# The order of ScalarE's second phase in a causal attention: the outputs' copy and the turned half's copy each go one place ahead

## The reference, cut to what matters

```
q, k, v per head (16 heads of 64), v and k from a latent of 64; rotary on q and k
scores = q @ k.T / 8, causal mask
probs  = softmax(scores)
out    = probs @ v                  # per head
x      = layernorm(x + out @ wo)
```

## Time and profile before

| | us |
|---|---|
| median of three runs | 1637.8 (1637.06 to 1641.13) |
| profiled execution | 1635.31 |
| its span, first to last instruction | 1633.2 |
| TensorE busy in the span | 1504.0 (92%) |
| VectorE, ScalarE busy | 1146.4 (70%), 1087.7 (67%) |
| GpSimd busy | 523.0 (32%) |
| TensorE busy between 41 and 434 us, steps 1 to 30 of the first attention | 375.77 of 393 |

### The profile page before, as it was taken

The page is one execution under the profiler, slowest core; times in us unless marked ns, Lnnn a source line. Parts: engine busy times, 40 slices in busy tenths (PEclk is TensorE's granted clock), DMA queues, the critical chain, the costliest instruction groups (busy, mean ns, idle before and its releaser), DMA issues. The chain is left out here.

```text
span 1633.2 us, 30449 instructions
## 1 busy us (share of the span) xinstructions
PE 1504.0 (92%) x9934; PEld 1018.6 (62%) x9934; DVE 1146.4 (70%) x2592; ACT 1087.7 (67%) x2499; POOL 523.0 (32%) x476
## 2 busy tenths in 40 slices
PE   7999999999979999999998999997999988999986
PEld 6777777777657888888863333333666655566654
DVE  2677777676657777777787888864777753777755
ACT  3565665656567888888865777754778754787852
POOL 1222222222231122221110000014777733677732
PEclk9999999999979999999997999977999998999998
DMA  7000000000002212212100000000000000000000
GB/s 244 2 2 1 0 0 0 0 0 0 1 28 80 78 64 77 76 52 77 65 1 1 1 1 1 1 1 0 2 1 1 1 1 0 1 2 1 1 1 26
DMA packets 18849, 36.54 MB, mean 22 GB/s; under 512 B 5492, under 2 KB 10736, under 8 KB 16560
## 3 DMA queue, kind: packets, MB, share of 16 engines
q1 hardware_dynamic: 18752, 35.29, 6.4%
HBM read 34.10 MB, written 1.18 MB: 22 GB/s over the span
## 5 line engine op out<-in xcount | busy, mean ns | idle before, releaser
L915 DVE TENSOR_TENSOR m_hidp<-m_hid,m_hidp 128x512 fp32r<-128x512 f32 x256 | 178.2, 722 | 77.9 <-ACT m_hidp L831 76.6
L305 ACT ACTIVATE a_prob<-a_prob,a_negmax 128x512 f32<-128x512 f32 (+3 forms) x256 | 142.2, 556 | 135.9 <-DVE a_negmax L382 135.9
L836 ACT ACTIVATE m_hid<-ps,pre_w 128x512 f32<-128x512 f32 x256 | 175.3, 685 | 63.5 <-PE ps L1064 62.7
L1064 PE MATMUL ps<-c_sb_st,m_w1p 128*128 128x512 f32 x768 | 191.4, 398 | 0.0
L1119 PE MATMUL ps<-m_hidp,m_w2p 128*128 128x512 f32 x768 | 190.0, 396 | 0.2 <-DVE m_hidp L915 0.2
L1441 ACT ACTIVATE c_sb_pT<-ps 128x512 f32<-128x512 f32 x256 | 137.4, 601 | 70.7 <-PE ps L1654 69.7
L265 POOL TENSOR_TENSOR a_qk_r<-a_qk_c,a_qk_s 128x512 f32<-128x512 f32 x64 | 81.6, 1275 | 318.6 <-DVE a_qk_s L372 318.6
L1511 DVE TENSOR_REDUCE c_sb_negmax<-ps 128x1 f32<-128x512 f32 x240 | 152.5, 685 | 38.9 <-PE ps L1639 38.9
L1064 PEld LDWEIGHTS ps<-c_sb_st,m_w1p 128*128 128x128 f32 x768 | 144.7, 189 | 37.9 <-issue 3.0
L1119 PEld LDWEIGHTS ps<-m_hidp,m_w2p 128*128 128x128 f32 x768 | 144.1, 188 | 35.8 <-DVE m_hidp L915 0.4
L2038 ACT ACTIVATE l_sb_prob<-ps,l_sb_negmax,l_sb_rn 128x192 f32<-128x192 f32 (+1 forms) x256 | 124.1, 499 | 47.9 <-DVE l_sb_negmax L2140 47.9
(11 more groups left out here) (246 smaller groups left out, 3198.5 us busy)
## 6 DMA issues: line engine op xcount, KB each, us to landing
m_gate_all<-m_gates_d SPq DMA_DIRECT2D x16, 1024.0 KB, 4.6
pre_w<-w1T SPq DMA_DIRECT2D x14, 258.0 KB, 2.7
pre_w<-w2T SPq DMA_DIRECT2D x14, 256.0 KB, 2.8
pre_wqkv<-wqkv SPq DMA_DIRECT2D x2, 768.0 KB
keep_x<-x SPq DMA_DIRECT2D x1, 1024.0 KB, 9.4
out<-keep_x SPq DMA_DIRECT2D x4, 256.0 KB, 2.3
keep_xT<-xT SPq DMA_DIRECT2D x1, 768.0 KB, 6.8
pre_m_w<-l_w SPq DMA_DIRECT2D x2, 341.0 KB
```

What stands on the lines that cost most here:

```text
L305: nc.scalar.activation(prob[:, u % 4, 0:width(p)], prob[:, u % 4, 0:width(p)], ACT.Exp, scale=-1.0, bias=negmax[:, u:u + 1], accum_out=den ...
L836: nc.scalar.activation(hid[:, c % 2, f, :], ps[:, f, :], ACT.Gelu, bias=w1[:, k, FF + f:FF + f + 1]).then_inc(gelu_done, 1)
L915: nc.vector.tensor_tensor(hidp[:, c % 2, 1, f, :], hid[:, c % 2, f, :], hidp[:, c % 2, 0, f, :], ALU.subtract).then_inc(low_done, 1)
L1064: ins = nc.tensor.matmul(ps[:, f, :], w1p[:, k, a, f * P:(f + 1) * P], xp[:, b, c, :], start=(i == 0), stop=(i == 2))
```

## The change

In ScalarE's list, in the part of the second phase, copy_o of the step before goes ahead of exp(1, 0), and copy_pT(n, 0) ahead of exp(1, 1). The lists of the other engines are as they were.

```
-            exp(n, b, 1, 0)
             if later(n):
                 copy_o(n - 1)
+            exp(n, b, 1, 0)
+            copy_pT(n, 0)
             exp(n, b, 1, 1)
-            copy_pT(n, 0)
```

## The result

| | before | changed |
|---|---|---|
| median of six runs, us | 1638.49 (1635.82 to 1641.13) | 1618.12 (1615.85 to 1625.85) |
| profiled execution, span | 1633.2 | 1613.7 |
| a step in the loop | 13.18 | 12.52 |
| TensorE's listed pauses in 30 steps | 17.2 | none at line 500 |

The ratio is 0.9885, with a 95% interval of 0.9857 to 0.9913: 20.4 us faster by the medians, where 20.7 was the sum and 1617 the forecast.

A forecast was written before the change was run, and what follows sets the result against it. TensorE, busy 375.77 of 393 us, was taken to bound the first attention, with only its pauses to win. Terms of 16.1, 3.5, 0.5 and 0.6 give 20.7 us: 1637.8 - 20.7 = 1617, range 1612 to 1628.

The forecast's parts named there:

- the sum: First attention: 16.1 us in loop steps, 3.5 in straight steps, 0.5 in the first, 0.6 in the last; together 20.7.
- the pause: First attention: TensorE waits before the value matmuls, line 500; 30 listed pauses, 17.2 us, expected to go whole.
- The rival that the pause was not ScalarE's: Line 500: the listed releaser is only "issue" and VectorE's copy is also awaited; no gain, 1638 us, chance 0.06.
- The warning that 0.04 rests on a modelled end: copy_o's start, 0.04 us after TensorE's values, counts from a matmul end computed from size, not observed.
- Both slacks: ScalarE, second phase: copy_o has 0.26 us to spare before exp(1,0); copy_pT(n, 0) is ready 0.41 before TensorE.
- The next tight place: copy_pT(n, 1) before its value matmuls: bound by exp(2,1), which does not move; 0.33 us left.
- the bracket: Recorded pauses before line 500, 0.59 and 0.50 us, smaller than by starts; they would sum to 18.2 us, 1619.6.
- The first step: First attention step, which has no copy_o: the pause at the value matmuls goes, 0.51 us.
- The last step: Last attention step, no projections: copy_pT decides and moves ahead by the exponential taken out before it, 0.59 us.
- the loads had long landed: Stages after the attention: DMA share 0.00 over the attention, so what is won there is carried to the end.

The follow-up runs named there:

- three copies: Changed kernel with two more copies of the outputs, into buffers that nothing reads, ahead of copy_o; median 1630.84 us, ratio 0.9955 to the kernel before.
- Two and three copies: Changed kernel with the outputs copied twice or three times, the extra copies ahead of copy_o and read by nothing; medians 1618.59 and 1630.84 us.
- two half edits: Kernel before with only copy_pT(n, 0) moved ahead of exp(1,1), ratio 0.9889, or only copy_o moved ahead of exp(1,0), ratio 0.9924.

## Why the prediction was right

**The releaser of the pause.** The profile said "issue"; the prediction named ScalarE's copy from 0.10 between its end and TensorE's start. Where this copy was the last to come, that distance held in all experiments: 0.10 with only the second exchange, 0.11 with only the first, 0.10 with three copies. The rival that the pause was not ScalarE's fell with the changed kernel's own profile.

**The first exchange costs nothing.** copy_o starts 0.04 after the values, as read from the one row at the stage's end, and exp(1, 0) still starts 0.04 after VectorE's maximum. The warning that 0.04 rests on a modelled end was fair; 0.03 to 0.05 came out in every step.

**Both slacks.** 0.41 before TensorE is ready: measured 0.42. The next tight place, 0.33: measured 0.35. Two and three copies put the edge on either side of the sum.

**The pause measured by starts, not by the bracket.** 0.67 a loop step was forecast and 0.66 came, 20.4 us from the first step to the last where the brackets would have given 18.2. The two half edits show why the brackets mislead: pauses of 0.07 and 0.18 stand in no bracket.

**The terms.** The first step gave its 0.51 (1.14 to 0.63). The 30 steps after it gave 19.14 us (429.53 - 35.54 before, from the same timeline as the earlier trace rows, 410.48 - 35.63 now) where the sum had 19.6: 13.18, 12.52 and 0.63 are rounded, and 0.01 a step is 0.3 us of the 0.5. The last step gave 0.71 where 0.59 was forecast, from copy_pT starting 0.89 after scores(2) before and 0.18 now (421.06 against 420.88). There copy_o, now ahead of exp(1, 0), starts at once and need not wait for VectorE's maximum, for which exp(1, 0), then at the head, had waited: the forecast counted the exponential taken out, and missed this 0.1.

**What was carried to the end.** The attention's 20.4 us are the medians' 20.4. That is partly luck, as the six runs lie up to 10 us apart (below); by the ratio it is 18.8 us, with an interval from 14 to 23. One reason given for it, that the loads had long landed, rests on the DMA share in the attention and does not hold behind it: in the first 100 us of the next stage that share was 0.18 before and 0.17 now. These transfers did not hold the gain back, with 19.8 us at that stage's first matmul and 19.5 at the end.

## What to carry to other kernels

In an engine that works strictly in order, ask of each instruction who waits for it and when it can start. A copy that another engine waits for goes ahead of work that nobody needs yet, and a copy that must be done at some time goes where the engine is idle, if its release comes before that of the instruction behind it by more than its own length. Two such moves in front of one wait do not add up: the gain ends where the waiting engine is ready, which is read from the distances between its starts, not from its listed pauses.

## What the runs showed of the hardware

The runs of one kernel scatter by up to 15 us (three copies, 1623.90 to 1638.69), though the attention steps of the changed kernel agree to 0.01 us in its two profiled executions. In the profile of the second exchange alone (1625.4 us, against a median of 1619.9) the time after the attention was 9 us longer than in the changed kernel. The second attention holds it: its matmuls on line 1654 run from 849.5 to 1098.9 in the changed kernel and from 850.5 to 1108.4 there. Ten microseconds near its start, table by stretch, first the changed kernel, then the other, 1 us later on its clock and with the ten microseconds ahead:

```profile
866.00:876.00 10.00, 10.00 (x76) 3.84 (x76) 9.08 (x16) 7.57 (x15) 0.29 (x1) 1.00 0.01 2
```

```profile
857.00:867.00 10.00, 9.70 (x70) 5.98 (x70) 7.58 (x14) 9.35 (x18) 0.53 (x2) 0.99 0.00 0
867.00:877.00 10.00, 10.00 (x56) 2.79 (x53) 6.82 (x11) 5.38 (x10) 0.00 (x0) 0.66 0.01 2
```

From 866 or 867 us on TensorE is busy throughout in both, but at a mean granted clock of 0.66 instead of 1.00 it gets 56 matmuls done instead of 76. The clock there had already risen, to 0.99 from 857 to 867 us with TensorE busy for 9.70 of the 10, and fell again: in stretches of 2 us it is 0.50, the lower of its two levels (1.2 GHz of 2.4), from 868 to 874 us. Such falls come in the changed kernel too, the first after this rise at 896 to 898 us. Over the first 50 us of this part (from 836.33 and 837.15) the mean clock was 0.82 in the changed kernel and 0.73 in the other. This is the same program part in both kernels; why the clock falls at one time in one run and at another in the next stays open.

It is one source of the scatter, not shown to be all of it. Of the six runs of the changed kernel the two of 1625 to 1626 us have a mean clock of 0.952 and the four of 1616 to 1619 have 0.958 to 0.961; but with three copies runs of 1623.9 and of 1630.3 us both have 0.961. It means that a change of under some 5 us in this kernel is better read from the steps in a profile than from the time.
